# Feed-forward's first layer by seven products instead of eight, on pairs of chunks

## The chip, the cores and the metric

The kernel runs on one core of a Trainium2 chip. The metric is the device time in microseconds of one execution; before the change it is 3593.21 us (median of three runs, 3593.11 to 3593.33).

## The reference

Two gated layers on a batch of 16 sequences of 256 rows, width 512; the context has 256 rows of width 256. All is float32. The first layer is a cross-attention of 16 heads and a routed feed-forward of 8 experts; the second a normed cross-attention of 16 heads and a plain feed-forward with 2048 hidden columns. The last of the four lines is the one that the change is about:

```python
x = x + jnp.tanh(g_xattn[0]) * _L0_xattn_ref(_layernorm(x), ctx_1024, ...)
x = x + jnp.tanh(g_ffn[0]) * _L0_ffn_ref(_layernorm(x), ...)
x = x + jnp.tanh(g_xattn[1]) * _L1_xattn_ref(_layernorm(x), ctx_1024, ...)
x = x + jnp.tanh(g_ffn[1]) * _L1_ffn_ref(_layernorm(x), ...)

def _L1_ffn_ref(x, proj1, proj1_bias, proj2, proj2_bias, gate_w):
    h = jax.nn.gelu(jnp.einsum('lne,he->lnh', x, proj1) + proj1_bias, approximate=False)
    return jnp.einsum('lnh,eh->lne', h, proj2) + proj2_bias
```

## The kernel before

Four stages run one after another, each a function with its own prefix on tile names: `a_` (cross-attention and routing, 0 to about 1490 us), `e_` (experts, to about 2110 us), `d_` (normed attention, to about 2866 us) and `f_` (the last feed-forward, to the end). Every product is made of three matmuls in fp32r (`three`): each operand is split in a high part (a cast to fp32r on ACT) and a low part (value minus high part, a subtraction on DVE or POOL), and high times high, low times high and high times low are summed in PSUM.

**The feed-forward** (`feed_forward`, from L2462) walks over 8 chunks of 512 rows (`CH`). The hidden layer has 16 tiles of 128 columns (`HC`). For tile j of a chunk, `hidden` makes x times w1, transposed, in one bank `f_hb` (4 blocks of the width times 3 matmuls of 128x512, L2571 to L2573), ACT applies the gelu into `f_h_f` (L2635) and casts the high part (L2637), DVE subtracts for the low part (L2676), and `out` adds the tile's share of the second layer to four banks `f_ob` (4 blocks of rows times 3 matmuls). So a tile is 24 matmuls. PE's order is hidden(j+1), out(j); each engine's queue is in program order, and semaphores tie the engines. Rows of the next chunk are normed and turned (16 transposes through `f_tb`, L2579) while the chunk runs. All weights stay in SBUF, split at the stage's start.

**The first stage** (from L69) is a pipeline of 256 heads' steps; a step is one call of `step(f, u)` on each engine, some 4.4 to 6 us long, 8 to a batch and a half of the heads, 16 to one turn of the loop. In a step PE makes the queries (`a_pj`), the scores (`a_sc`), the values (`a_avb`), the projection (`a_ob`) and last turns the probabilities of two steps ago into the single bank `a_ptb` (L574), for which it waits until DVE has taken the low part of what the bank held (`a_pt_lo`, L851). ACT casts `a_pt_hi` (L734) first, then the query (L729), the exponentials (L740) and `a_ot_hi` (L749), and last what the batch shares: x, keys, values, and in every eighth step the context (`a_ctx`, L765). POOL scales the probabilities (L815) and in every eighth step takes a root (L820). SP loads and stores rows. ACT's queue also issues stores of blanks to `x_sorted` (L773).

Of the kernel before, what the change touches and what calls it, by code (L numbers as in the profile page):

```python
# [9 lines left out]
ALU = mybir.AluOpType  # L10
ACT = mybir.ActivationFunctionType
AX = mybir.AxisListType
P = 128
# [11 lines left out]
SLOTS = 42 * 7 * P  # L25
MADE = (2, 3, 4, 5)
# [43 lines left out]
def gated_cross_attention_and_route(nc, x_in, x_half, x_out, xt_rows, ctx_rows, x_sorted, y_sorted, tile_table, table, tab_loaded, weights, slots, listed, w_gate, wkv, kv_made, kv_kept, ident, in_hi, in_lo, ctx_t, mask, gate, wq, wk, wv, wo,  # L70
# [13 lines left out]
    with ExitStack() as ctx:  # L84
# [106 lines left out]
        kv_ctx, kv_zero, kv_ready, kv_taken = [sem(f"kv_ctx{j}") for j in range(len(MADE))], sem("kv_zero"), sem("kv_ready"), sem("kv_taken")  # L191
        o_ready, o_free, x_stored = sem("o_ready"), sem("o_free"), [sem("x_stored0"), sem("x_stored1")]
# [108 lines left out]
        def all_steps(eng, step):  # L301
# [3 lines left out]
            with eng.Fori(1, half - 1) as i:  # L305
                for u in range(AHEAD, AHEAD + PAIR):
                    step((i, 1, half - 2), u)
            for u in range(AHEAD, AHEAD + PAIR):
                step((half - 1, half - 1, half - 1), u)
# [21 lines left out]
        def kv_out(n):  # L331
            return prob[:, n % 4].rearrange("p t s -> p (t s)")

# [38 lines left out]
        def _(sp):  # L372
# [43 lines left out]
            def step(f, u):  # L416
# [45 lines left out]
                for n in splits(f, u):  # L462
                    if SET + 3 <= n + 3 < 2 * SET:
                        load(n + 3)
                at_step = last_steps(f, u)
# [19 lines left out]
            all_steps(sp, step)  # L485
            for n in (*KV_MORE, *KV_REST[:2]):
                keep_kv(n)
# [208 lines left out]
        def _(act):  # L696
# [34 lines left out]
            def step(f, u):  # L731
# [28 lines left out]
                for bb in context(f, u):  # L760
# [4 lines left out]
                    nc.scalar.copy(ctx_hi, ctx_raw[:]).then_inc(c_hid, 1)  # L765
                for n in splits(f, u):
                    split(n)
                for to, first, steps in ((x_sorted, 1, FILL), (y_sorted, B // 2 + 1, FILL_LATER)):
                    if f[1] == first and f[2] > first and u in steps:
# [34 lines left out]
        def _(pool):  # L804
# [5 lines left out]
            def step(f, u):  # L810
# [14 lines left out]

                if f[1] == f[2] and PAIR * f[1] + u == 117:
                    pool.wait_ge(pj_ready, number[B - 1, "x1"] + 1)
                    nc.gpsimd.memset(ones, 1.0).then_inc(ones_set, 1)
# [826 lines left out]

def gated_normed_attention(nc, x_in, y_sorted, weights, slots, x_out, ctx_rows, kv_made, kv_kept, dca_hi, dca_lo, kv_dca, gate, ln_cols, ident, raw_in, raw_out, in_hi, in_lo, after, ahead, tag):
# [11 lines left out]
    with ExitStack() as ctx:  # L1668
# [15 lines left out]
        y_sb = sb("y_sb", [P, 2, TOPK, D])  # L1684
# [42 lines left out]
        ff_loaded, ff_x_loaded = [sem("ff_loaded0"), sem("ff_loaded1")], sem("ff_x_loaded")  # L1727
# [103 lines left out]
        def _(sp):  # L1831
# [1015 lines left out]
```

## Time and profile before

| | us |
|---|---|
| median of three runs | 3593.21 |
| the profiled execution's own time | 3592.75 |
| its span | 3590.8 |
| PE busy (share of the span) | 3500.4 (97%) |
| DVE, ACT, POOL busy | 2166.8, 1824.2, 1461.9 |

The mean granted clock is 0.991 of full speed. A row of the timeline gives the start, the duration, the engine, the line, the operation, what it writes and reads, and in square brackets the idle time of the engine before it and who ended it. `<-` stands between output and input.

### The profile page before, as it was taken

Reading aid. Unit: us, or ns where it says so; the run is one execution under the profiler, and the core shown is the slowest. Engines: PE = TensorE matmul, PEld = TensorE weight load, DVE = VectorE, ACT = ScalarE, POOL = GpSimd, SP = SyncE. Lnnn points to the kernel's source line nnn. Section 1 sums busy time; section 2 is a strip of 40 time slices with the busy share of each in tenths; the row PEclk is TensorE's granted clock in tenths of the full one; section 3 lists DMA queues with packets and bytes.
Section 4 is the critical chain, followed back from the end, with each engine's and each line's share of the span. In section 5 each row is a group of like instructions: output and inputs, shape, how many; then the busy total and the mean of one; then the engine's idle time right before and its main releaser. Section 6 shows DMA issues by size and latency. Waiting matters only on the chain. (4 is left out here: it accounts for less than half of the span.)

```text
span 3590.8 us, 65577 instructions
## 1 busy us (share of the span) xinstructions
PE 3500.4 (97%) x22678; PEld 3030.6 (84%) x22678; DVE 2166.8 (60%) x5435; ACT 1824.2 (51%) x4724; POOL 1461.9 (41%) x1484
## 2 busy tenths in 40 slices
PE   9999999999999999899999997999999899999999
PEld 8999999999999998699999985667777588888887
DVE  6666666656666666577777777787777542222221
ACT  5444454554444444455555554787777732222222
POOL 4333333443444444354455545777777430000000
PEclk9999999999999999999999998999999999999999
DMA  4466666325666664577777662222221120000000
GB/s 166 171 226 226 225 219 219 137 95 190 219 219 222 220 220 142 201 257 256 264 261 255 248 236 94 83 81 66 63 66 64 43 84 24 24 24 24 24 24 24
DMA packets 232438, 530.18 MB, mean 148 GB/s; under 512 B 12929, under 2 KB 29442, under 8 KB 228098
## 3 DMA queue, kind: packets, MB, share of 16 engines
q1 hardware_dynamic: 131714, 314.14, 25.4%
q10 hardware_dynamic: 90208, 179.32, 13.5%
q0 software_dynamic: 10272, 33.63, 2.8%
q8 instruction: 134, 2.20, 0.3%
q14 instruction: 110, 0.90, 0.1%
HBM read 273.28 MB, written 253.76 MB: 147 GB/s over the span
## 5 line engine op out<-in xcount | busy, mean ns | idle before, releaser
L815 POOL TENSOR_SCALAR a_prob<-a_prob,a_rinv 128x256 f32<-128x256 f32 x512 | 472.4, 934 | 827.7 <-DVE a_rinv L1021 827.4
L740 ACT ACTIVATE a_prob<-a_prob,a_low_bias 128x256 f32<-128x256 f32 x512 | 256.4, 502 | 465.9 <-DVE a_low_bias L1012 465.9
L2635 ACT ACTIVATE f_h_f<-f_hb,ff_consts 128x512 f32<-128x512 f32 x128 | 88.3, 690 | 456.1 <-PE f_hb L2573 452.1
L500 PE MATMUL a_pj<-a_xt,in_hi 128*128 128x256 f32 x1024 | 309.9, 303 | 0.1
L1326 POOL TENSOR_TENSOR e_act_hi<-e_act_f,e_zeros 128x256 fp32r<-128x256 f32 x128 | 181.6, 1419 | 310.8 <-DVE e_act_f L1541 310.8
L1340 PE MATMUL e_gb<-e_xt_hi,in_hi 128*128 128x256 f32 x1024 | 291.6, 285 | 3.0 <-DVE e_xt_lo L1520 3.0
L1341 PE MATMUL e_gb<-e_xt_lo,in_hi 128*128 128x256 f32 x1024 | 290.7, 284 | 0.0
L1342 PE MATMUL e_gb<-e_xt_hi,in_lo 128*128 128x256 f32 x1024 | 290.7, 284 | 0.0
L502 PE MATMUL a_pj<-a_xt,in_lo 128*128 128x256 f32 x1024 | 289.1, 282 | 0.0
L501 PE MATMUL a_pj<-a_xt,in_hi 128*128 128x256 f32 x1024 | 288.9, 282 | 0.0
L851 DVE TENSOR_TENSOR a_ot_lo<-a_avb,a_ot_hi 128x256 fp32r<-128x256 f32 x256 | 108.3, 423 | 256.7 <-ACT a_ot_hi L749 256.7
L2184 POOL TENSOR_TENSOR raw_in<-raw_in,d_rinv 128x480 f32<-128x480 f32 x256 | 254.8, 1015 | 0.0
L1520 DVE TENSOR_TENSOR in_lo<-raw_in,in_hi 128x1024 fp32r<-128x1024 f32 (+1 forms) x160 | 205.4, 1288 | 60.9 <-ACT in_hi L1424 60.2
L2088 ACT ACTIVATE raw_in<-d_sc,d_nmax 128x240 f32<-128x240 f32 x512 | 232.9, 478 | 0.0
L2098 ACT COPY d_pt<-d_ptb 128x512 f32<-128x512 f32 x256 | 154.4, 603 | 118.4 <-PE d_ptb L1983 118.4
L851 DVE TENSOR_TENSOR a_pt_lo<-a_ptb,a_pt_hi 128x512 fp32r<-128x512 f32 x256 | 175.5, 686 | 51.6 <-ACT a_pt_hi L734 36.0
L2653 POOL TENSOR_TENSOR f_rstd<-f_var,f_power 128x4 f32<-128x4 f32 x7 | 7.0, 1006 | 486.7 <-DVE f_var L2700 486.7
L500 PE MATMUL a_ob<-in_hi,a_ot_hi 128*128 128x512 f32 x512 | 202.6, 396 | 2.6 <-POOL in_lo L824 1.9
L501 PE MATMUL a_ob<-in_lo,a_ot_hi 128*128 128x512 f32 x512 | 202.3, 395 | 0.0
L1340 PEld LDWEIGHTS e_gb<-e_xt_hi,in_hi 128*128 128x128 f32 x1024 | 197.5, 193 | 4.5 <-DVE e_xt_lo L1520 3.6
L502 PE MATMUL a_ob<-in_hi,a_ot_lo 128*128 128x512 f32 x512 | 199.7, 390 | 0.0
L1341 PEld LDWEIGHTS e_gb<-e_xt_lo,in_hi 128*128 128x128 f32 x1024 | 197.5, 193 | 0.9
(455 smaller groups left out, 11362.2 us busy)
## 6 DMA issues: line engine op xcount, KB each, us to landing
raw_in<-in_w_gate SPq DMA_DIRECT2D x39, 2048.0 KB, 8.6
x_sorted<-a_spare ACTq DMA_DIRECT2D x42, 1792.0 KB, 6.5
y_sorted<-a_spare ACTq DMA_DIRECT2D x42, 1792.0 KB, 8.8
raw_out<-in_w_out SPq DMA_DIRECT2D x40, 1024.0 KB, 5.4
xt_rows<-a_xt SPq DMA_DIRECT2D x16, 1024.0 KB, 5.4
a_xt<-xt_rows SPq DMA_DIRECT2D x16, 1024.0 KB, 5.2
e_xg<-x_sorted SPq DMA_DIRECT2D x32, 512.0 KB, 9.3
y_sorted<-e_y_sb SPq DMA_DIRECT2D x32, 512.0 KB, 2.9
```

The lines of the kernel that those rows point to most:

```text
L500: nc.tensor.matmul(out, a_hi, b_hi, start=start, stop=False)
L501: nc.tensor.matmul(out, a_hi, b_lo, start=False, stop=False)
L502: return nc.tensor.matmul(out, a_lo, b_hi, start=False, stop=stop)
L740: e = nc.scalar.activation(prob[:, u % 4, t], prob[:, u % 4, t], ACT.Exp, bias=low_bias[:, u % 2, t:t + 1], scale=-1.0, accum_out=rsum[:, ...
L815: p = nc.gpsimd.tensor_scalar(prob[:, u % 4, t], prob[:, u % 4, t], rinv[:, u % 2, t:t + 1], None, ALU.mult)
L851: return nc.vector.tensor_tensor(out, raw_in, hi.bitcast(F32), ALU.subtract)
L1340: nc.tensor.matmul(out, a_hi, b_hi, start=start, stop=False)
L1341: nc.tensor.matmul(out, a_hi, b_lo, start=False, stop=False)
L1342: return nc.tensor.matmul(out, a_lo, b_hi, start=False, stop=stop)
L1520: return nc.vector.tensor_tensor(out, raw, hi.bitcast(F32), ALU.subtract)
L2088: e = nc.scalar.activation(p[:, j, t, DCA:], s[:, j, t * S + DCA:(t + 1) * S], ACT.Exp, bias=nmax[:, n % 2, 1, 2 * j + t:2 * j + t + 1], a ...
L2184: T(p[:, j, :, DCA:], p[:, j, :, DCA:], r[:, 1, 2 * j:2 * j + 2].unsqueeze(2).to_broadcast([P, 2, S - DCA]), ALU.mult).then_inc(p_done, 1)
```

## The change

It splits both matrices of the first layer in halves of rows, width and hidden columns and makes the eight half products with seven (the scheme of Strassen in Winograd's form): 7 products of half the width for a tile of two hidden tiles and two chunks. The stage walks over 4 pairs of chunks (`PAIRS`) and 8 tiles j (`JC`) of a pair. For each (pair, j) PE makes seven `product`s of 2 x 3 matmuls into four banks of the tensor `turned`; ACT copies the first from PSUM (`snap`), DVE makes seven additions (`hidden`), ACT four gelus. The hidden tiles of the pair's first chunk go to `out` between the products; those of the second chunk are kept in SBUF and go to `out` when the first chunk is done. Four operands made of sums of x (T1 to T4) are made once a pair: `sums` on DVE, high parts on ACT, low parts on POOL and DVE.

The seven operands of w1 are made in the first stage, in 16 units of 64 columns (`prepared`): SP loads at step 4, 9 or 14 of a turn of the loop, POOL makes four sums one step later, ACT casts two steps later, POOL subtracts three steps later, SP stores four steps later to the DRAM tensor `w1_ops`. Three units fall into each of the five turns of the loop and one into the steps before it; the sixth turn, which was in the loop, is now written out. In the feed-forward SP loads each operand tile of each (pair, j, product) from `w1_ops` into a ring of 8 places, two transfers of 128 KB; the first eight places are filled in the attention. There the piece of w1 that was split ahead is gone, and the rows of the second chunk are loaded and normed ahead. All loops of the feed-forward are written out.

The diff, cut to its core; its pieces are, in order, `prepared`, then SP (two loops), ACT and POOL (two loops) of the first stage, then SP's `load_op` and PE's `hidden` (removed), `product` and main loops of the feed-forward:

```diff
+        def prepared(f, u, after):
+            if f[2] < B // 2 - 2 and f[1] >= 1:
+                return [at(f, lambda k: 3 * k - 2 + (u - after - AHEAD) // 5)] if u - after in (AHEAD, AHEAD + 5, AHEAD + 10) else []
+            return [0] if f[2] == 0 and u - after == 12 else []
...
+                for n in prepared(f, u, 0):
+                        sp.wait_ge(part_lod, n)
+                    for h in range(2):
+                        sp.dma_start(part_raw[:, h], w1[:, :, bass.ds(n * UNIT + h * H1 // 2, UNIT)]).then_inc(part_loaded, 16)
+                for n in prepared(f, u, 4):
+                    sp.wait_ge(part_lod, n + 1)
+                    for h, rows_of in enumerate((part_hi, part_lo)):
+                        sp.dma_start(w1_ops.rearrange("o c p h n -> p (o c) h n")[:, :, h, bass.ds(n * UNIT, UNIT)],
+                                     rows_of.rearrange("p (a n) -> p a n", a=14)).then_inc(part_kept, 16)
...
+                for n in prepared(f, u, 2):
+                    act.wait_ge(part_link, 3 * n + 3)
+                        act.wait_ge(part_kept, 32 * n)
+                    for of, to in part_of:
+                        h = nc.scalar.copy(part_hi[:, to].bitcast(F32R), w_raw[:].rearrange("p a b -> p (a b)")[:, of])
...
+                for n in prepared(f, u, 1):
+                    pool.wait_ge(part_loaded, 32 * n + 32)
+                    nc.gpsimd.tensor_tensor(part_sum[:, 0], a21, a22, ALU.add)
+                    nc.gpsimd.tensor_tensor(part_sum[:, 2], a11, a21, ALU.subtract).then_inc(part_link, 1)
+                    ...
+                for n in prepared(f, u, 3):
+                    pool.wait_ge(part_hid, n + 1)
+                    for of, to in part_of:
+                        l = nc.gpsimd.tensor_tensor(part_lo[:, to].bitcast(F32R), w_raw[:].rearrange("p a b -> p (a b)")[:, of], part_hi[:, to], ALU.subtract)
...
+            def load_op(n):
+                sp.wait_ge(p_ready, n - RING + 1)
+                for half, room in enumerate((ahead.ring_hi, ahead.ring_lo)):
+                    sp.dma_start(room(slot).bitcast(F32), w1_ops[op, :, :, half, j * P:(j + 1) * P].rearrange("c p n -> p c n")).then_inc(ring_loaded[slot], 16)
...
-            def hidden(n, b, j):
-                for c in range(FC):
-                    mm = three(hb[j % 2][:], w_hi[of][:, c, cols], w_lo[of][:, c, cols], xt_hi[b][:, c], xt_lo[b][:, c], c == 0, c == FC - 1)
+            def product(p, j, i):
+                if n >= RING:
+                    pe.wait_ge(ring_loaded[n % RING], 32 * (n // RING))
+                if j == 0:
+                    wait_op(p, i)
+                if i < 4 and g:
+                    pe.wait_ge(added, ADDS * (g - 1) + (3, 6, 7, 5)[i])
+                elif i == 4:
+                    pe.wait_ge(snapped, g + 1)
+                elif i > 4:
+                    pe.wait_ge(added, ADDS * g + i - 4)
+                for c in range(2):
+                    mm = three(out, hi[:, c], lo[:, c], x_hi[i][:, c], x_lo[i][:, c], c == 0, c == 1)
...
+            turn(rows_next, ob)
+            for i in range(N):
+                product(0, 0, i)
+            for p in range(PAIRS):
+                for j in range(1, JC):
+                    for i in range(5):
+                        product(p, j, i)
+                    out(p, 0, 2 * j - 2)
+                    product(p, j, 5)
+                    product(p, j, 6)
+                    out(p, 0, 2 * j - 1)
+                out(p, 0, HC - 2)
+                out(p, 0, HC - 1)
+                for k in range(HC):
+                    out(p, 1, k)
...
```

In the last loop PE also turns rows at k 1 and 7 and makes products of the next pair's first tile at k 13 and 14. `part_of` are two spans, of 256 and 640 columns: one unit of 64 columns is 14 such pieces for the seven operands.

What stands in ACT's row in the first stage around the step in which the context is cast (`a_ctx`), before:

```order
L749 CAST a_ot_hi<-a_avb 128x256 [waits a_av_ready]
L761 REGISTER_ALU
L764 ISA [waits a_pj_ready,a_c_loaded0]
L765 CAST a_ctx<-a_spare 128x512 [waits a_c_kept]
L734 CAST a_pt_hi<-a_ptb 128x512 [waits a_t_ready]
```

and now, in the loop's step 16:

```order
L780 CAST a_ot_hi<-a_avb 128x256 [waits a_av_ready]
L795 REGISTER_ALU [waits a_pj_ready,a_c_loaded1]
L796 CAST a_ctx<-a_spare 128x512 [waits a_c_kept]
L798 ISA
L801 REGISTER_ALU [waits a_part_link]
L804 CAST a_w_raw<-a_w_raw 128x256 [waits a_part_kept]
L804 CAST a_w_raw<-a_w_raw 128x640
L765 CAST a_pt_hi<-a_ptb 128x512 [waits a_t_ready]
```

Between the context's cast and the cast of the turned probabilities ACT now waits for POOL's sums (`a_part_link`) and for the stores of the unit before (`a_part_kept`), and makes two casts. POOL one step earlier, step 15, before:

```order
L815 TENSOR_SCALAR a_prob<-a_prob,a_rinv 128x256 [waits a_r_done]
L815 TENSOR_SCALAR a_prob<-a_prob,a_rinv 128x256
L818 ISA
L820 TENSOR_TENSOR a_columns<-a_columns,a_power 128x2 [waits a_stat_link]
L812 REGISTER_ALU
L815 TENSOR_SCALAR a_prob<-a_prob,a_rinv 128x256 [waits a_r_done]
```

and now:

```order
L855 TENSOR_SCALAR a_prob<-a_prob,a_rinv 128x256
L858 REGISTER_ALU
L860 TENSOR_TENSOR a_columns<-a_columns,a_power 128x2 [waits a_stat_link]
L867 ISA
L870 TENSOR_TENSOR a_w_raw<-a_w_raw 128x128 [waits a_part_loaded]
L871 TENSOR_TENSOR a_w_raw<-a_w_raw 128x128
L872 ISA
L873 TENSOR_TENSOR a_w_raw<-a_w_raw 128x128 [waits a_part_link]
L874 REGISTER_ALU
L875 TENSOR_TENSOR a_w_raw<-a_w_raw 128x128 [waits a_part_link]
```

The four sums stand behind the root and ahead of the next scaling. SP's row in steps 8 and 9 of the loop now reads:

```order
L490 REGISTER_ALU
L493 DMA w_ops<-a_w_raw 128x14x64 [waits a_part_lod]
L493 DMA w_ops<-a_w_raw 128x14x64
L412 REGISTER_ALU
L415 ISA [waits a_c_lod]
L415 DMA ctx_rows<-a_ctx 128x1024
L488 ISA [waits a_part_lod]
L488 DMA a_w_raw<-in_w 128x4x64
L488 ISA
L488 DMA a_w_raw<-in_w 128x4x64
```

Of these ten rows only the context's store (L415; L396 to L399 before) was there; the stores of one unit stand ahead of it and the loads of the next behind it.

## Rows read from the trace of the kernel before

**Rows 1.** Page, part 1: busy us, share, instructions of each engine

```profile
PE 3500.4 (97%) x22678; PEld 3030.6 (84%) x22678; DVE 2166.8 (60%) x5435; ACT 1824.2 (51%) x4724; POOL 1461.9 (41%) x1484
```

**Rows 2.** Windows: busy us (instructions) of each engine, then clock, DMA share, GB/s

```profile
300.00:600.00 300.00, 300.00 (x2152) 280.58 (x2151) 190.72 (x603) 149.25 (x430) 107.23 (x116) 1.00 0.63 226
3000.00:3200.00 200.00, 200.00 (x905) 165.55 (x904) 52.22 (x90) 53.03 (x82) 2.01 (x2) 1.00 0.06 22
```

**Rows 3.** Timeline, PE, steady feed-forward: start, duration, engine, line, operation

```profile
2887.71 0.39 PE L2571 MATMUL f_hb<-in_hi 128*128 128x512 f32 x1
...
2893.15 0.39 PE L2571 MATMUL f_hb<-in_hi 128*128 128x512 f32 x1
```

**Rows 4.** Waits, 2880 to 3591 us: total, times, longest

```profile
ACT f_h_f L2635 <- PE f_hb L2573: 447.9, 124, 4.8
```

**Rows 5.** Lines by form, 2890 to 3591 us: busy, mean ns | idle before

```profile
L2635 ACT ACTIVATE f_h_f<-f_hb,ff_consts 128x512 f32<-128x512 f32 x125 | 86.2, 690 | 450.0 <-PE f_hb L2573 446.0 <-DVE dca_lo L2676 4.0
```

**Rows 6.** Timeline, start of the feed-forward, 2871 to 2885 us

```profile
2871.47 0.63 PE L2572 MATMUL f_hb<-in_lo,in_hi 128*128 128x512 f32 x1
2871.90 0.63 PE L2573 MATMUL f_hb<-in_hi,in_lo 128*128 128x512 f32 x1
...
2879.64 4.62 POOL L2657 TENSOR_TENSOR in_lo<-raw_in,in_hi 128x2048 fp32r<-128x2048 f32 x1 [8.94 <-ACT in_hi L2624]
...
2880.76 4.05 DVE L2676 TENSOR_TENSOR f_h_lo<-f_h_f,f_h_hi 128x512 fp32r<-128x512 f32 x1 [2.36 <-ACT f_h_hi L2637]
...
2884.86 0.50 PE L2571 MATMUL f_ob<-in_hi,f_h_hi 128*128 128x512 f32 x1 [0.39 <-DVE f_h_lo L2676]
```

**Rows 7.** Timeline, first stage, 551 to 556 us, four engines

```profile
552.04 0.62 ACT L765 CAST a_ctx<-a_spare 128x512 fp32r<-128x512 f32 x1
552.56 0.58 ACT L734 CAST a_pt_hi<-a_ptb 128x512 fp32r<-128x512 f32 x1
...
551.20 1.82 POOL L815 TENSOR_SCALAR a_prob<-a_prob,a_rinv 128x256 f32<-128x256 f32 x2 [5.42 <-DVE a_rinv L1021]
552.99 0.97 POOL L820 TENSOR_TENSOR a_columns<-a_columns,a_power 128x2 f32<-128x2 f32 x1
...
553.30 0.68 DVE L851 TENSOR_TENSOR a_pt_lo<-a_ptb,a_pt_hi 128x512 fp32r<-128x512 f32 x1
...
555.28 0.60 PE L574 MATMUL a_ptb<-ident,a_prob 128*128 128x128 f32 x4
```

**Rows 8.** Timeline, POOL and PE, first stage, two other steps

```profile
537.89 1.82 POOL L815 TENSOR_SCALAR a_prob<-a_prob,a_rinv 128x256 f32<-128x256 f32 x2 [4.29 <-DVE a_rinv L1021]
...
545.89 0.60 PE L574 MATMUL a_ptb<-ident,a_prob 128*128 128x128 f32 x4
...
564.53 1.82 POOL L815 TENSOR_SCALAR a_prob<-a_prob,a_rinv 128x256 f32<-128x256 f32 x2 [2.82 <-DVE a_rinv L1021]
...
571.67 0.60 PE L574 MATMUL a_ptb<-ident,a_prob 128*128 128x128 f32 x4
```

**Rows 9.** Lines by form, POOL, whole span

```profile
L1328 POOL TENSOR_TENSOR e_act_lo<-e_act_f,e_act_hi 128x256 fp32r<-128x256 f32 x128 | 148.6, 1161 | 10.0
L2197 POOL TENSOR_TENSOR raw_in<-raw_in,d_hrstd 128x512 f32<-128x512 f32 x64 | 67.6, 1057 | 11.3 <-DVE d_hrstd L1825 11.3
...
L2182 POOL TENSOR_TENSOR raw_in<-raw_in,d_rinv 128x64 f32<-128x64 f32 x128 | 56.9, 445 | 158.8 <-DVE d_rinv L2408 157.7 <-POOL d_x_sb L2206 0.3
```

**Rows 10.** DMA: 682 to 683.5 us (1 KB packets), 3000 to 3088 us

```profile
DMA packets 480, 0.55 MB, mean 365 GB/s; under 512 B 9, under 2 KB 471, under 8 KB 471
...
q1 hardware_dynamic: 480, 0.55, 104.8%
...
q1 hardware_dynamic: 1056, 2.10, 6.7%
```

**Rows 11.** DMA issues, 590 to 614 us: KB each, us to landing

```profile
x_sorted<-a_spare ACTq DMA_DIRECT2D x3, 1792.0 KB, 6.5
```

More of the change, by code:

```diff
@@ L25 @@
 SLOTS = 42 * 7 * P
+NUNITS = 16
 MADE = (2, 3, 4, 5)
@@ L2525, in all_chunks @@
-        def all_chunks(eng, chunk):
-            for b in range(2):
-                chunk(0, b, False, b == 0)
-            with eng.Fori(1, CHUNKS // 2 - 1) as i:
-                for b in range(2):
-                    chunk(i, b, False)
-            for b in range(2):
-                chunk(CHUNKS // 2 - 1, b, b == 1)
+        credit = sb("credit", [P, 2])
+        b1_sb, gate_t = ahead.b1_sb, ahead.gate_t
+        rows = [ahead.x_first, ahead.xn, raw_in[:, 0, :, 0:D], raw_in[:, 0, :, D:2 * D]]
@@ L2568, in _ @@
+            store(2 * PAIRS - 1, other(PAIRS - 1))
+            sp.wait_ge(x_stored[0], 16 * PAIRS)
+            for n in (1, 2):
+                sp.wait_ge(x_stored[n], 16 * (PAIRS // 2))
         @block.tensor
@@ L2643, in _, with split, snap, gelu_of @@
-            all_chunks(act, chunk)
+            def split(m):
+                act.wait_ge(w_loaded, 32 * m)
+                nc.scalar.copy(w2_hi[:, m - 1], w2_raw).then_inc(w_hid, 1)
+            def snap(g):
+                act.wait_ge(p_ready, N * g + 1)
+                if g:
+                    act.wait_ge(gelu_done, 4 * g)
+                nc.scalar.copy(part[0], lw[:, BANK[0]]).then_inc(snapped, 1)
+            def gelu_of(g, n):
+                p, j = divmod(g, JC)
+                act.wait_ge(added, ADDS * g + (1, 4, 6, 7)[n])
+                if p == 0 and j == 4 and n == 1:
+                    act.wait_ge(w_lod, 3)
+                to, of = ((part[3], part[3]), (kept[JC + j], part[1]), (part[2], part[2]), (kept[j], part[0]))[n]
+                tile = j + JC * (n in (1, 2))
+                nc.scalar.activation(to, of, ACT.Gelu, bias=b1_sb[:, tile:tile + 1]).then_inc(gelu_done, 1)
@@ L2659, in chunk, with low_op @@
[L2659 to L2669 removed]
+            def low_op(p, i):
+                for c in range(2):
+                    pool.wait_ge(op_hid, 10 * p + {T1: 5, T3: 7, T4: 9}[i] + c)
+                    T(x_lo[i][:, c], raw_of[i][c], x_hi[i][:, c].bitcast(F32), ALU.subtract).then_inc(op_lod_pool, 1)
@@ new lines, in residual @@
+            def residual(n):
+                to, loads = (0, n // 2) if n % 2 == 0 else (other(n // 2), n // 2 + 1)
+                if n:
+                    pool.wait_ge(rows_loaded[to], 16 * loads)
+                for t in range(TC):
+                    r = T(rows[to][:, t], rows[to][:, t], b2_sb[:], ALU.add)
+                r.then_inc(res_done, 1)
+            def root(n):
+                pool.wait_ge(link_done, 3 * n + 3)
+                T(rstd[:], var[:], power[:], ALU.pow).then_inc(root_done, 1)
@@ new lines, in normalize @@
+            def normalize(n, x, tiles):
+                if tiles[0] == 0:
+                    dve.wait_ge(root_done, n + 1)
+                for t in tiles:
+                    l = V.tensor_scalar(rows[x][:, t], rows[x][:, t], mv[:, t, 0:1], rstd[:, t:t + 1], ALU.subtract, ALU.mult)
+                if tiles[-1] == TC - 1:
+                    l.then_inc(xn_done, 1)
+            sums(0, T1)
+            sums(0, T2)
+            low_op(0, T2)
+            sums(0, T4)
+            sums(0, T3)
```

710 lines of the change are left out of this document (461 added, 249 removed).

## The prediction

> **What bounds the kernel now.** I read the page's busy line first: PE is busy 97% of the span, 3500.4 of 3590.8 us, the next engine 60% [rows 1]. So time comes from fewer matmuls, and is lost by making PE wait. Then the windows, to see which stages have room. In 300 to 600 us, the first stage, PE is busy 300.00 of 300.00; DVE 191, ACT 149, POOL 107 [rows 2]. There a helper may grow in the mean, but every microsecond by which one comes late is a microsecond of the end, since PE has no idle time to give back. In 3000 to 3200 us, the feed-forward, PE is again busy for all of it and DVE, ACT and POOL 52, 53 and 2 us; the DMA share is 0.06 [rows 2]. The timeline gives the rate: one tile, 24 matmuls, starts at 2887.71 and the next at 2893.15, 5.44 us, 0.2267 us a matmul [rows 3]. The waits say who waits: ACT's gelu 447.9 us for PE's `f_hb` [rows 4], and no stop of PE in the windows. The feed-forward is the matmuls' time.
>
> **The products.** Before, 8 chunks x 16 tiles x 12 matmuls = 1536. Now 4 pairs x 8 tiles x 7 products x 6 = 1344. The second layer and the 16 transposes of each chunk stay. 192 fewer x 0.2267 [rows 3] = **-43.5 us**. Both forms are 128x512, and the clock is at full speed in the whole window [rows 2].
>
> What is added beside them: for each of 32 (pair, j) seven additions on DVE, one copy and four gelus and casts on ACT. An addition that reads PSUM is not there; the nearest row is the subtraction `a_pt_lo`, one input in PSUM, same size, 0.68 us [rows 7]. 224 x 0.69 = 155 us on DVE. A first-half group of PE is 42 + 24 = 66 matmuls, 15.0 us; DVE has 7 additions, 2 low parts of the tiles for the first chunk and 2 for the second: 11 x 0.69 = 7.6 us. ACT has 5 operations of 0.69 [rows 5] and four casts of 0.6, 5.9 us. Both fit twice over. By latency: a product of 6 matmuls is 1.36 us, an addition 0.68 us and some 0.1 of signal, and a bank is asked for again three or four products later. I take 0; if one addition a group is missed by 0.3 us it is 32 x 0.3 = 10 us, the upper end.
>
> **The ring.** 224 operand tiles, each 2 transfers of 256 packets of 512 B. No row shows 512 B. 480 packets of about 1 KB took 104.8% of 16 engines for 1.5 us, 52 ns each; 1056 of 2 KB took 6.7% of 88 us, 89 ns [rows 10]. By a straight line 512 B is about 34 ns, bounds 26 (half of 52) and 52. A tile needs 512/16 x 34 = 1.1 us (0.8 to 1.7) and PE gives it 15.0/7 = 2.1 us in a first half, and none are asked for in most of a second half (eight lie ready). I take 0, since even the upper end is below 2.1.
>
> **The start of the feed-forward.** Before: PE takes up the first tile at half pace (0.43 us from one matmul to the next [rows 6]) and stops 0.39 us for `f_h_lo`, which took DVE 4.05 us beside POOL's 4.62 us split of 128x2048 [rows 6], plus a few tenths at the turn. Now four operands are made one after another, DVE's sums, ACT's cast, the low part on POOL or DVE, some 1.2 us each in turn, while PE has a product of 1.36 us for each: I count stops of 0.8 + 1.3 + 1.3 + 0.8 = 4.2 us against about 1. **+3**, from -1 (the stop for `f_h_lo` goes too) to +8 (matmuls stay at half pace for another 40, 40 x 0.2). In the later pairs the operands are made behind 12 `out`s.
> The row shows 4.05 us for a 128x512 subtraction that takes 0.68 elsewhere, while POOL works: the Trainium skill says in the GPSIMD Engine Reference, section Specifications, that GPSIMD shares its SBUF interfaces with VectorE, with contention where DVE has two SBUF inputs. That speaks against the change, which adds POOL work in the first stage and keeps DVE's two-input subtractions; by it each POOL sum of a unit may hold a DVE operation up by its own 0.5 us. It is inside the lateness counted below: DVE's `a_pt_lo` reads one input from PSUM.
>
> **The first stage: the weights' units.** A unit has a part on POOL, ACT and POOL again, at three consecutive steps; three units to a turn of the loop, 5 turns, 15 units and one before. What decides is who stands behind. ACT's two casts stand ahead of `a_pt_hi`, behind that is DVE's `a_pt_lo`, and PE's `a_ptb` waits for it.
>
> Where the context is cast too (step 16 of the loop), before: POOL's scaling ends 551.20 + 1.82 = 553.02, the root at 553.96; ACT's context cast starts 552.04, `a_pt_hi` 552.56, DVE's `a_pt_lo` runs 553.30 to 553.98, and PE asks at 555.28 [rows 7]: a margin of 1.3 us. Now the four sums of 128x128 follow POOL's root. Nearest rows: 0.445 us for 128x64, 1.057 for 128x512 [rows 9]; by a straight line 128x128 is 0.53. Four, with waits between, 2.2 us (1.8 to 4.2): ready at 556.2. ACT casts 256 and 640 columns; 128x512 takes 0.62 [rows 7], so 1.1 us with the fixed part twice: 557.3. `a_pt_hi` 0.58: 557.9. `a_pt_lo` 0.68: 558.6, against 555.28: 3.3 us, and about 0.5 for what `a_ot_lo`, queued behind on DVE, holds up. 3.8 x 5 turns = **+19** (12 to 30).
>
> At the other two places there is no root. Step 6: scaling ends 537.89 + 1.82 = 539.71, sums 541.9, casts 543.0, `a_pt_lo` 544.3; PE asks at 545.89 [rows 8]: hidden by 1.6 us. Step 11: 564.53 + 1.82 + 2.2 + 1.1 + 1.3 = 570.9, PE at 571.67 [rows 8]: hidden by 0.8. With the sums at the upper end (the 128x512 row, 4.2 us) both are late, by 0.4 and 1.2, 5 x 1.6 = 8 us.
>
> **The loads behind stores.** SP stores a unit at the step before the next one is loaded: 2 transfers of 1792 packets of 256 B, then the context's store, then the loads, 1024 packets of 256 B. Meanwhile ACT's queue sends 1792 KB of blanks, which land after 6.5 us [rows 11]. With 24 ns for 256 B (half the step below 34; bounds 13 and 52): stores 3584/16 x 24 = 5.4 us, loads 1.5, context 512 KB about 1.5, blanks 5 at the full rate of the row: 13.4 us of queue, and the sums ask some 10 us after the issue. Late by 2 to 4.5 us less the margin of 0.8: I take 2 a turn, **+10** (0 if the queues are served by turns and the load is let through; 7 x 5 = 35 at 52 ns).
> The rows have no packet under 1 KB in numbers. The Trainium skill, DMA: Bandwidth & Descriptors, Specifications, gives 512 B as the least transfer for line rate, and below it a read-modify-write; the change's stores are below. Twice the price for the stores would be an estimated 5 us more a turn, +25.
>
> **The rest.** The attention (`d_`) loses its w1 splits and gets the second chunk's norm: DVE about +3, ACT -2, beside PE's products: 0 (-2 to +3). The loops written out: 0, since PE's instructions are issued from the same queue; no row shows a cost of a longer program.
>
> **Sum.** 3592.75 - 43.5 + 3 + 19 + 10 = 3581.2 in the profile's own time, which was 0.46 below the median of the runs: **3582**.
>
> **Rivals.**
> *H, the first stage hides it.* PE's queue runs ahead of `a_ptb` little, but the sums may be cheaper or POOL may be earlier than in the turn I read. Then 5 to 15 us are left of 29: 3592.75 - 43.5 + 3 + (0 to 15) + 0.5 = 3553 to 3568. For it: 107 of 300 us on POOL [rows 2]. Against it: PE has no slack, and `a_pt_lo` has 1.3.
> *S, slower.* The stores of 256 B and the loads behind them make every unit late. POOL's sums then stand ahead of the next scaling, and all of the chain is late by the DMA. It decides from a lateness of 8 us more than my 2, at the two places behind a store in a turn: 10 x 5 us + 19 = 69, time 3592.75 - 43.5 + 3 + 69 + 0.5 = 3622. Range 3601 to 3630. For it: the share of DMA is already 0.63 there [rows 2]. Against: 0.37 is free, and a unit has 5 steps.
> *D, the ring bounds PE.* If a tile's load takes more than 2.1 us (over 67 ns a packet of 512 B, or 1.07 us for the issue of each transfer on SP), the gain shrinks by 224 x the excess: at 2.4 us 224 x 0.3 = 67 us less in the first halves, 3600 to 3640. Against: both packet rows.
> *N, the products do not shorten the stage*, since a product of six matmuls waits each time for its bank: four stops of 0.3 us in each of 32 groups, 38 us; 3592.75 - 43.5 + 38 + 32 + 0.5 = 3620. The margins above speak against.
>
> **Chances.** Forecast 0.50 (its own range 3568 to 3592), H 0.27, S 0.14, D and N together 0.09. What a measurement of this kernel can tell from no change is 0.2%, 7.2 us: faster is below 3586.0, slower above 3600.4. The forecast's case is below 3586 seven times in ten, 0.35, the rest within 0.2%; with H faster is 0.62; S and D and N give slower 0.18 (part of their 0.23 stays within); same 0.20. Range: 0.1 to be left out at each side: 3556 to 3606.
>
> **What would show it.** The stage from the first `f_` matmul to the end shortens by some 40 us. PE's idle time ahead of the transposes to `a_ptb`, released by DVE's `a_pt_lo`, is 3 to 4 us at step 16 in each of five turns and under 0.5 at step 6. POOL's wait for `part_loaded` exists at one or both places behind a store. PE's waits for the ring are nought, and it has four stops at the start of the feed-forward. The forecast is wrong if PE waits for `added` or `snapped` in the groups, or if the idle time at `a_ptb` is not by these three steps.

## The result: 0.2% slower, and where the time went

The median of eight runs is 3603.95 us (3597.51 to 3608.60) against 3594.69 us (3593.11 to 3599.43) of the kernel before on the same chip; the ratio of the runs is 1.0022, with a 95% interval of 1.0013 to 1.0031. The forecast was 3582 and faster; the range 3556 to 3606 holds the time. The profiled execution took 3598.05 us (span 3596.2), 5.3 more than that of before.

| | before | after |
|---|---|---|
| first matmul of the experts | 1498.89 | 1548.38 |
| first matmul of the feed-forward | 2870.91 | 2917.60 |
| end | 3590.8 | 3596.2 |
| first stage | 1498.9 | 1548.4 (+49.5) |
| experts and second attention | 1372.0 | 1369.2 (-2.8) |
| feed-forward | 719.9 | 678.6 (-41.3) |

The stage borders are rows of the timeline, of before and of after (start, duration, engine, line, operation, in brackets the idle time of PE and who ended it):

```profile
1498.89 1.33 PE L1352 MATMUL e_tb<-ident,e_xg 128*128 128x128 f32 x5 [8.23 <-DMA e_xg<-x_sorted]
...
2870.91 0.77 PE L2571 MATMUL f_hb<-in_hi 128*128 128x512 f32 x1 [4.68 <-DVE f_credit L2680]
```

```profile
1548.38 1.97 PE L1408 MATMUL e_tb<-ident,e_xg 128*128 128x128 f32 x8 [6.18 <-DMA e_xg<-x_sorted]
...
2917.60 3.65 PE L2683 MATMUL f_ob<-ident,rows_next 128*128 128x128 f32 x16 [4.39 <-PEq L67]
...
2927.29 0.50 PE L2676 MATMUL turned<-in_hi 128*128 128x512 f32 x1 [1.18 <-POOL in_lo L2882]
...
2930.24 0.50 PE L2676 MATMUL turned<-f_op_hi,in_hi 128*128 128x512 f32 x1 [1.28 <-POOL f_op_lo L2882]
...
2932.90 0.50 PE L2676 MATMUL turned<-f_op_hi,in_hi 128*128 128x512 f32 x1 [1.03 <-POOL f_op_lo L2882]
```

The last three rows are the stops at the start of the feed-forward, 3.5 us for the sums of x. PE makes 22486 matmuls in place of 22678, the 192 fewer that were forecast, and is busy 97% of the span as before. The windows of after, which answer to [rows 2] (us busy of PE, of its weight loads, DVE, ACT and POOL, then granted clock, DMA share, GB/s):

```profile
3000.00:3200.00 200.00, 200.00 (x901) 166.06 (x900) 97.72 (x158) 65.81 (x106) 20.77 (x16) 1.00 0.43 127
405.03:411.30 6.27, 6.27 (x46) 5.76 (x47) 4.38 (x18) 3.04 (x11) 2.62 (x3) 1.00 0.00 0
565.57:572.63 7.06, 6.63 (x46) 5.99 (x47) 5.24 (x18) 2.77 (x9) 1.83 (x2) 1.00 0.87 335
178.21:185.90 7.69, 7.69 (x46) 7.43 (x47) 5.41 (x19) 3.39 (x11) 2.12 (x3) 0.78 0.78 299
500.30:508.04 7.74, 7.74 (x39) 7.43 (x40) 4.90 (x19) 3.56 (x12) 3.54 (x4) 0.63 0.00 0
600.00:604.00 4.00, 4.00 (x20) 4.00 (x19) 2.75 (x9) 2.21 (x7) 2.10 (x2) 0.50 0.00 0
```

In 3000 to 3200 us PE is as full as before; DVE went from 52 to 98 us and the DMA share from 0.06 to 0.43, and neither is felt. The other windows are the 6 to 8 us behind a stop in the first stage: the column ahead of the DMA share is the granted clock, and it is 1.00 in two of them, 0.78 and 0.63 in two, and 0.50, the lower of the two levels (1.2 and 2.4 GHz), in 600 to 604 us. A mean between 0.50 and 1.00 is a share of the window at each level. Who waits there, in the waits of PE from 150 to 640 us (total, times, longest):

```profile
PE a_ptb L605 <- DVE a_pt_lo L907: 29.4, 10, 5.0
PE a_ob L531 <- DVE a_xo_sb L1093: 0.4, 1, 0.4
```

The kernel before has no wait of PE in this stretch. There are ten stops at `a_ptb`, two to a turn. One kind is at step 16; here that of turn 2 on four engines:

```profile
303.17 0.97 POOL L860 TENSOR_TENSOR a_columns<-a_columns,a_power 128x2 f32<-128x2 f32 x1
304.11 0.46 POOL L870 TENSOR_TENSOR a_w_raw<-a_w_raw 128x128 f32<-128x128 f32 x1
...
305.61 0.45 POOL L875 TENSOR_TENSOR a_w_raw<-a_w_raw 128x128 f32<-128x128 f32 x1
...
306.28 1.03 ACT L804 CAST a_w_raw<-a_w_raw 128x256 fp32r<-128x256 f32 x2 [3.45 <-POOL a_w_raw L875]
307.22 0.58 ACT L765 CAST a_pt_hi<-a_ptb 128x512 fp32r<-128x512 f32 x1
...
307.83 0.69 DVE L907 TENSOR_TENSOR a_pt_lo<-a_ptb,a_pt_hi 128x512 fp32r<-128x512 f32 x1 [4.27 <-ACT a_pt_hi L765]
...
308.66 1.09 PE L605 MATMUL a_ptb<-ident,a_prob 128*128 128x128 f32 x4 [3.06 <-DVE a_pt_lo L907]
```

Root to 304.1, four sums to 306.1, two casts to 307.3, `a_pt_hi`, `a_pt_lo` to 308.5, and PE, which asked at 305.6, goes on at 308.66. This is the chain that was forecast from [rows 7]. The other kind is at step 11, where ACT's casts wait for the sums that POOL makes at its step 10 (POOL and SP, turn 2):

```profile
256.67 2.27 POOL L880 TENSOR_TENSOR a_w_raw<-a_w_raw 128x256 fp32r<-128x256 f32 x2
...
271.73 0.46 POOL L870 TENSOR_TENSOR a_w_raw<-a_w_raw 128x128 f32<-128x128 f32 x1 [2.96 <-DMA a_w_raw<-in_w]
...
259.08 4.24 SPq L493 DMA_DIRECT2D w_ops<-a_w_raw  x2
263.63 3.39 SPq L415 DMA_DIRECT2D ctx_rows<-a_ctx  x1
267.25 1.89 SPq L488 DMA_DIRECT2D a_w_raw<-in_w  x2
```

The low parts are done at 258.9. SP issues the stores for 4.24 us and the context's store for 3.39, and gets to the loads at 267.25; POOL has waited 2.96 us for them when the first sum begins at 271.73.

Set against the kernel before transpose by transpose (the start of each `a_ptb` group in both traces), the five turns lost 46.4 us, each time at these two places, and nothing at step 6:

| turn | step 11: stop, loss there, loss in the next step | step 16: the same |
|---|---|---|
| 1 | 2.44, 2.60, 1.55 | 4.56, 4.72, 1.53 |
| 2 | 2.04, 2.21, 1.52 | 3.06, 3.20, 1.34 |
| 3 | 2.06, 2.21, 1.54 | 3.05, 3.21, 0.28 |
| 4 | 2.07, 2.23, 1.48 | 3.05, 3.21, 2.61 |
| 5 | 2.07, 2.23, 0.93 | 5.01, 5.15, 2.61 |

The stops are 29.4 us. Another 17.0 us, over a third, were lost besides: 1.6 at the place itself and 15.4 in the step behind. The rows say how:

```profile
405.61 0.28 PE L532 MATMUL a_pj<-a_xt,in_hi 128*128 128x256 f32 x1
405.73 0.28 PE L533 MATMUL a_pj<-a_xt,in_lo 128*128 128x256 f32 x1
407.32 0.42 DVE L907 TENSOR_TENSOR a_ot_lo<-a_avb,a_ot_hi 128x256 fp32r<-128x256 f32 x1 [1.14 <-ACT a_ot_hi L780]
407.80 0.38 PE L531 MATMUL a_avb<-a_pt_hi,a_v_hi 128*128 128x256 f32 x1
...
600.40 0.41 PE L532 MATMUL a_pj<-a_xt,in_hi 128*128 128x256 f32 x1
600.61 0.41 PE L533 MATMUL a_pj<-a_xt,in_lo 128*128 128x256 f32 x1
```

- The 1.6 us, 0.16 a stop, come from how idle time is counted. A matmul row of 128x512 lasts 0.39 us while the next one starts 0.23 us behind it; the idle time counts from the row's end, 0.16 us later than PE could have gone on.
- Behind a stop at the lower level, two matmuls of 128x256 start 0.21 us apart (600.40 and 600.61) in place of 0.12 (405.61 and 405.73), so that 0.44 of each microsecond at that level is lost. The eight windows with a clock under 1.00 hold 31 us of it, which makes 14 us; these eight steps lost 14.2.
- Behind a stop at 1.00 a second, short wait follows. At 405.03 us PE goes on, and starts `a_avb` 2.77 us later, at 407.80, where it takes 2.58 us in the kernel before. DVE has just finished `a_ot_lo`, at 407.74: the late `a_pt_lo` made the scores' work on DVE late, this the exponentials on ACT, these `a_ot_hi`, and this `a_ot_lo`. The idle column does not show it, since it fits into the modelled length of the matmul before it. That is the 0.28; in the 0.93 of turn 5 there is also the wait of 0.4 us for `a_xo_sb`. At the lower level PE comes to `a_avb` 3.8 to 4.7 us behind the stop, when `a_ot_lo` is long done.

So the lower level took 14.2 of the 17.0 us. At full clock these steps would presumably have met the short waits instead; with 0.28 and 0.93 for them as in the two windows at 1.00, what the level added is some 9.3 us. Of the remaining 3.1 us of the first stage 2.9 are at its end, where PE stops 3.3 us for `a_xn`.

### The profile page after: what moved, and what is told of

The parts are those of the page before. It is cut to its first block and busy times, and to the rows that moved or that the text cites. A ratio compares the mean times of both kernels' runs of the same rounds, so it can differ in the third digit from the quotient of the medians.

```text
span 3596.2 us, 66239 instructions
## 1 busy us (share of the span) xinstructions
PE 3472.0 (97%) x22486; PEld 3009.8 (84%) x22486; DVE 2305.9 (64%) x5653; ACT 1867.4 (52%) x4821; POOL 1587.6 (44%) x1633
## 3 DMA queue, kind: packets, MB, share of 16 engines
q8 instruction: 135, 2.21, 0.2%
## 5 line engine op out<-in xcount | busy, mean ns | idle before, releaser
L531 PE MATMUL a_pj<-a_xt,in_hi 128*128 128x256 f32 x1024 | 313.6, 306 | 0.1
L532 PE MATMUL a_pj<-a_xt,in_hi 128*128 128x256 f32 x1024 | 292.4, 286 | 0.0
L2962 DVE TENSOR_TENSOR raw_in<-turned,raw_in 128x512 f32<-128x512 f32 x224 | 151.9, 690 | 212.7 <-PE turned L2678 209.8
L2158 ACT ACTIVATE raw_in<-turned,d_nmax 128x240 f32<-128x240 f32 x512 | 233.1, 478 | 0.0
L532 PEld LDWEIGHTS a_pj<-a_xt,in_hi 128*128 128x128 f32 x1024 | 199.1, 194 | 0.0
L531 PEld LDWEIGHTS a_pj<-a_xt,in_hi 128*128 128x128 f32 x1024 | 198.4, 194 | 0.5 <-DVE a_k_lo L907 0.5
```

Source lines behind the costliest of these rows:

```text
L531: nc.tensor.matmul(out, a_hi, b_hi, start=start, stop=False)
L532: nc.tensor.matmul(out, a_hi, b_lo, start=False, stop=False)
L2158: e = nc.scalar.activation(p[:, j, t, DCA:], s[:, j, t * S + DCA:(t + 1) * S], ACT.Exp, bias=nmax[:, n % 2, 1, 2 * j + t:2 * j + t + 1], a ...
```

## The experiments

**Without the units.** Theory A was that the units' lateness costs the first stage what the table shows; its rival was that the written-out program or the feed-forward's transfers cost something everywhere.

```diff
 def prepared(f, u, after):
-    if f[2] < B // 2 - 2 and f[1] >= 1:
-        return [...]
     return [0] if f[2] == 0 and u - after == 12 else []
```

> The changed kernel without the 15 units of w1 in the first stage's five turns: no loads, sums, casts, low parts or stores of them there. The one unit of the first turn stays and fills a small w1_ops of 128 columns, from which the feed-forward's ring loads every tile (same packets, other data). Theory A (the units' lateness costs the first stage its 46 us, by 29 us of stops of PE at a_ptb and 17 us of matmuls at the lower clock behind them): PE stops at a_ptb under 1 us in 150 to 640 us, clock 1.00 there, profiled time 3598 - 46 = 3549 to 3554, and the runs less scattered than the 3597 to 3609 of the changed kernel. Rival B (the written-out program, or the feed-forward's new transfers, slow everything a little): above 3575.

Measured: 3551.64 us, median of four runs (3549.62 to 3557.94), 0.9877 of before (0.9859 to 0.9894). PE has no wait in 150 to 640 us:

```profile
150.00:640.00 490.00, 490.00 (x3521) 458.54 (x3519) 313.95 (x993) 243.73 (x701) 174.95 (x188) 1.00 0.63 227
2872.80:3551.30 678.50, 668.80 (x2992) 554.40 (x2992) 330.09 (x523) 227.78 (x358) 95.72 (x66) 1.00 0.40 122
```

The 15 units cost 3598.05 - 3553.13 = 44.9 us between profiled executions. The medians of this section stand beside other runs of the kernel before, 3597.44 for this one and 3594.69 for the result above, so against these the units cost 52 to 55 us. The second row is the feed-forward, 678.5 us, for the next comparison. The four runs are less scattered than the eight of the changed kernel, by 8 us in place of 11, and not by much: the kernel before gave 3590.63 to 3600.43 here, the slower runs with a mean clock of 0.988, the fastest with 0.991.

**Without the ring's loads.** In `units_off`, `load_op` returns at once and PE waits only for the first eight tiles; all later products use these.

> units_off with the feed-forward's ring left as the first eight tiles filled it: no more loads of operand tiles in the feed-forward, PE waits for none. If the ring is hidden, as its waits of 0 on PE say, the time from the first f_ matmul to the end is that of units_off, 678.5 us, within 1 us. If the 56 MB that it moves slow the stage in a way that no wait shows, it is shorter by more.

```profile
2872.20:3550.80 678.60, 668.79 (x2992) 554.43 (x2992) 329.94 (x523) 227.69 (x358) 95.67 (x66) 1.00 0.11 38
```

678.6 us with a DMA share of 0.11, 678.5 with 0.40. The ring is free; the term of 0 for it was right.

**The casts a step later.**

```diff
-for n in prepared(f, u, 4):   # SP, stores
+for n in prepared(f, u, 5):
-for n in prepared(f, u, 2):   # ACT, casts
+for n in prepared(f, u, 3):
-for n in prepared(f, u, 3):   # POOL, low parts
+for n in prepared(f, u, 4):
```

> The changed kernel with each unit's casts on ACT, low parts on POOL and stores one step later; loads and sums stay. All the work and all the transfers are there, the output is the reference's. Theory A (the stop comes from what stands behind the wait for the sums): at the time of the cast the sums are a step old, so only the 1.05 us of casts stand ahead of a_pt_hi, the stops fall from 29 to under 3 us and the low clock goes with them: 3552 to 3560. Rival C (the added traffic and the ports hold the engines up, wherever the casts stand): 3585 or more, stops go on. Rival E (the low parts, now a step later on POOL, make the next unit's loads later still, and the sums hold the scalings up): 3565 to 3585.

Measured: 3555.31 us, median of four runs (3553.16 to 3557.51), 0.9882 of the kernel before (0.9866 to 0.9899). It is below the kernel before, 3597.44 beside it, by 42 us, and below the 3603.95 of the changed kernel by 49, with all transfers and all work of the units in it:

```profile
150.00:640.00 490.00, 490.00 (x3521) 458.55 (x3520) 320.99 (x993) 255.15 (x729) 232.40 (x274) 1.00 0.79 262
...
203.45 0.46 POOL L875 TENSOR_TENSOR a_w_raw<-a_w_raw 128x128 f32<-128x128 f32 x1
...
205.26 1.04 ACT L804 CAST a_w_raw<-a_w_raw 128x256 fp32r<-128x256 f32 x2 [0.87 <-DMA w_ops<-a_w_raw]
```

PE is busy 490.00 of 490 us at a clock of 1.00, with a DMA share of 0.79, where `units_off` has 0.63. So neither the added traffic nor POOL's added work beside DVE costs PE anything in this stretch. The last sum begins at 203.45 and the casts at 205.26; ACT waits 0.87 us for the stores of the unit before and for no sum, and the next `a_pt_hi` is still in time. What cost 46 us was where the waits stood. Two of them moved here: with the stores a step later, the loads of the next unit also stand ahead of them on SP. The next kernel has that alone; the casts moved alone were not run.

**The loads ahead of the stores.**

```diff
-for n in prepared(f, u, 4):   # SP, stores
+for n in prepared(f, u, 5):
```

> The changed kernel with the stores of a unit issued behind the loads of the next one instead of a step ahead of them; all else the same. The loads of the sums of step 10 are no longer behind 4.3 us of issuing of stores on SP. Theory A: POOL's 2.96 us of wait at step 10 is gone, with it the 2.1 us stop of PE and the 1.5 us behind it, five times 3.6 = 18; at step 15 the 1.5 and 1.95 us of load waits go, about 3 + 2: 3598 - 23 = 3575 (3570 to 3582), with five stops of 3.05 us left. Rival F (the loads are late by the share of the DMA engines, not by the queue's order): no change in the stops, 3595.

Measured: 3581.92 us (3578.70 to 3585.50), 0.9958 of before (0.9941 to 0.9975), at the upper end of what was expected; the profiled run 3582.56. SP and POOL at step 11 of turn 2, and PE's waits:

```profile
250.59 0.37 SPq L415 DMA_DIRECT2D ctx_rows<-a_ctx  x1
253.42 1.80 SPq L488 DMA_DIRECT2D a_w_raw<-in_w  x2
255.39 4.92 SPq L493 DMA_DIRECT2D w_ops<-a_w_raw  x2
...
262.99 0.46 POOL L870 TENSOR_TENSOR a_w_raw<-a_w_raw 128x128 f32<-128x128 f32 x1
```

```profile
PE a_ptb L605 <- DVE a_pt_lo L907: 15.2, 5, 3.0
```

The loads are issued at 253.4, ahead of 4.92 us of stores, and POOL no longer waits. All five stops at step 11 are gone, all five at step 16 are 3.05 us, and 9.7 us are lost behind them (2.57, 1.54, 1.46, 2.64, 1.53), more than I gave. Rival F is out. Of the 42 us that `cast_later` is below the kernel before, this order of loads and stores alone gives 15.5 and the later casts the other 27.

**Wider packets for the stores.**

```diff
-sp.dma_start(w1_ops.rearrange("o c p h n -> p (o c) h n")[:, :, h, bass.ds(n * UNIT, UNIT)],
-             rows_of.rearrange("p (a n) -> p a n", a=14))
+sp.dma_start(w1_ops...rearrange("(u p h a) -> u p h a", u=NUNITS, p=P, h=2)[bass.ds(n, 1), :, h]..., rows_of)
```

> The changed kernel, with each unit's parts stored as one row of 3584 B per partition in place of 14 pieces of 256 B (256 packets for 3584 a unit); the pieces then lie elsewhere in w1_ops, so the feed-forward's first layer multiplies with other numbers, in the same time. If the 256 B packets make the stores dear (the Trainium skill, DMA: Bandwidth & Descriptors, Specifications, puts the least size for line rate at 512 B), the issues of the stores on SP fall from 4.3 to under 1 us, the loads come early, the stops of 2.1 us at step 11 go, and 15 to 20 us with them: 3578 to 3583. If the order of the queue alone holds the loads up (the context's store and the blanks), the stops stay: 3595.

```profile
255.51 1.67 SPq L493 DMA_DIRECT2D w_ops<-a_w_raw  x2
257.50 0.97 SPq L415 DMA_DIRECT2D ctx_rows<-a_ctx  x1
258.70 2.45 SPq L488 DMA_DIRECT2D a_w_raw<-in_w  x2
...
266.24 0.45 POOL L870 TENSOR_TENSOR a_w_raw<-a_w_raw 128x128 f32<-128x128 f32 x1 [1.11 <-DMA a_w_raw<-in_w]
```

Measured: 3584.46 us in one run, the kernel before beside it 3593.41. The stores' issues take 1.67 us for 4.24 and the context's store behind them 0.97 for 3.39; POOL waits 1.11 us for 2.96, and PE's stop at step 11 is 0.18 us in turns 2 to 5 (1.09 in turn 1). The time is 1.5 us above what was expected, and the issues did not fall under 1 us. The same 896 KB in packets of 256 B hold SP's queue up by 5 us more than in packets of 3584 B, which is what the Trainium skill's page leads one to expect (DMA: Bandwidth & Descriptors, Specifications: line rate from 512 B on); the trace does not show its read-modify-write, only the time. The order of the queue and the size of the packets are two ways to the same 2 us.

**Stops without the units.** The kernel before was delayed on ACT alone. A first version (`late_three`) had a wrong bound on the loop, so that none of its copies were made; it is one more run of the kernel before, 3591.83 us. Its expectation was:

> The kernel before the change, with a_pt_hi copied 10, 12 and 13 times more at steps 7, 12 and 17 of each of the five turns, so that PE waits at a_ptb without any transfer, POOL or DVE work more. By the margins of 3.7, 3.9 and 1.3 us and 0.48 us a copy PE should stop 1.1, 1.9 and 4.9 us, 39.5 us in all. Theory A (a long stop itself lowers the clock behind it): behind the 1.9 us stop 1.5 us more are lost and behind the 4.9 us stop 1.5 to 2.6, behind the 1.1 us stop less or nothing; 3593 + 39.5 + 15 to 22 = 3648 to 3656. Rival C (what was lost behind the stops came from the units' traffic and engine work): only the stops, 3631 to 3636, and a clock of 1.00 behind them.

The mended one:

```diff
+for m in range(extra[u]):     # ahead of the copy of a_pt_hi, ACT
+    nc.scalar.copy(pt_hi[:, (u - 3) % 2], ptb[:]...).then_inc(again, 1)
+    act.wait_ge(again, ...)
```

> The kernel before the change, with a_pt_hi copied 7, 8 and 9 times more (each copy waiting for the one before by a semaphore, some 0.7 us each) at steps 7, 12 and 17 of the six turns of the loop, so that PE stops at a_ptb with no transfer and no POOL or DVE work more. By the margins of 3.7, 3.9 and 1.3 us the stops should be about 1.1, 1.8 and 5 us. Theory A (a stop of PE itself is followed by matmuls at the lower clock): behind the stops near 2 and near 5 us another 1.5 to 2.6 us are lost, with a granted clock under 0.8 in the next 6 us; behind the short one less or nothing. Rival C (what was lost behind the stops came from the units' traffic and engine work): the loss is the stops alone and the clock stays at 1.00 behind them.

```profile
179.50:186.60 7.10, 6.64 (x47) 6.03 (x48) 5.25 (x18) 2.72 (x9) 1.83 (x2) 1.00 0.80 210
212.90:219.60 6.70, 6.70 (x39) 6.40 (x40) 4.37 (x18) 3.55 (x12) 3.06 (x4) 0.75 0.00 1
...
PE a_ptb L575 <- DVE a_pt_lo L859: 49.4, 24, 4.6
```

Measured: 3674.19 us in one run, the kernel before beside it 3593.41. Behind each of the six stops of 4.63 us the next step lost 1.57 to 2.66 us; the window from 212.9 us has the clock at 0.75 with no transfer at all (DMA 0.00). A clock of 0.75 over 6.70 us is 3.4 us at the lower level, which at 0.44 is 1.5 of the 1.57 lost there. Behind the stops of 1.81 us it lost 0.92 to 0.95, the clock stays at 1.00 (window from 179.5), and 0.4 of it is a short wait for `a_xo_sb`. Behind those near 0.9 us 0.28. So the clock falls behind a stop without the traffic; rival C is out. The sizes match those of the changed kernel.

> The same kernel and the same kind of delay, but 3 to 7 copies more at eight steps of each of the six turns (5, 7, 9, 11, 13, 15, 17, 19), so that PE stops eight times for some 1 us instead of once for 5. If the clock falls only behind a long stop, the loss is the sum of the stops (about 45 us) and the clock stays at 1.00 in 100 to 650 us. If any idle share brings it down, it falls here as well and the loss is half as much again (65 us or more).

```profile
PE a_ptb L575 <- DVE a_pt_lo L859: 71.6, 60, 2.7
...
137.00:242.00 105.00, 92.60 (x632) 82.51 (x632) 55.23 (x179) 66.10 (x168) 31.69 (x34) 1.00 0.52 189
242.30:249.80 7.50, 7.50 (x41) 6.96 (x42) 4.55 (x18) 4.04 (x13) 3.66 (x4) 0.79 0.65 245
```

Measured: 3696.57 us in one run, stops of 0.72 to 1.70 us and, not meant so, one of 2.6 to 2.7 in turns 2 to 6. Neither expectation holds. In 137 to 242 us, with ten stops of 0.72 to 1.70 us, the clock stays at 1.00: idle share alone (PE is busy 93 of 105 us) does not bring it down. It falls behind the 2.60 us stop (0.79, and 1.47 us lost). Yet, set transpose by transpose as above, the six turns lost 103.9 us for 71.6 us of stops. The three terms found in the changed kernel account for it: 60 x 0.16 = 9.4 for the counting, 6.7 in the five steps at the lower level, and 0.28 in each of the other 55 steps (0.43 in five), 16.2. With the stops that is 103.9. In these steps PE starts `a_avb` 2.76 to 2.93 us behind the stop in place of 2.58, in most of them 0.05 us after DVE's `a_ot_lo` ends.

**The casts behind `a_pt_hi`.** ACT's block of `prepared(f, u, 2)` at the end of a step becomes `prepared(f, u, 3)` between the casts of `a_pt_hi` and `a_q_hi`.

> The changed kernel with one thing moved: on ACT a unit's casts, with their waits, stand behind the next a_pt_hi instead of ahead of it, and so ahead of the query's cast a_q_hi. Loads, sums, low parts and stores stay. Theory A (what stands behind the wait pays): the stops at a_ptb go (29 us, and 17 behind them), and a_q_hi and a_q_lo are late instead, which PE asks for at a_sc some 1.8 us after a_ptb. From the changed kernel's rows: casts end 597.9, a_q_hi and a_q_lo 0.8 later, PE would ask at 596.1, so 2.6 us where the loads are late (steps 15 of turns 1 and 5), 0.6 in the other three, and next to 0 at step 10: 7 us of stops, at most 5 behind them: 3598 - 46 + 7 to 12 = 3559 to 3564. Rival G (each place on ACT is as tight): the stops move to a_sc unshortened, 3590 or more.

```profile
PE a_pj L531 <- DVE a_q_lo L907: 20.7, 5, 5.6
PE a_avb L531 <- DVE a_ot_lo L907: 7.4, 5, 1.5
PE a_sc L531 <- DVE a_q_lo L907: 6.7, 5, 3.2
...
177.78 0.45 POOL L870 TENSOR_TENSOR a_w_raw<-a_w_raw 128x128 f32<-128x128 f32 x1 [7.56 <-DMA a_w_raw<-in_w]
```

Measured: 3616.17 us in one run, the kernel before beside it 3597.42. I was wrong by more than 50 us, and rival G's number holds. The stops at `a_ptb` are gone, but PE waits 34.8 us for the query and, which I had left out, for `a_ot_lo` behind it; and POOL waits 7.56 us for the loads of step 10. The later casts make the low parts later, and these the stores that stand ahead of the loads on SP. With the stores behind the loads:

> The same, and the stores of a unit behind the loads of the next one. The loads are then on time, and only the 0.6 us at step 15 are left, 3 us in all: 3552 to 3556, as cast_later. The output of both is the reference's.

```profile
PE a_avb L531 <- DVE a_ot_lo L907: 7.4, 5, 1.5
PE a_sc L531 <- DVE a_q_lo L907: 3.5, 5, 0.7
```

Measured: 3579.08 us (3575.29 to 3582.45), 0.9951 of before (0.9934 to 0.9967), 25 us above the forecast. The 0.70 us for the query are there, near the 0.6 expected, and 1.48 us more for `a_ot_lo` in each turn: the late query delays the exponentials, and `a_ot_hi` stands behind these on ACT. One step more of distance gives all of it back; a place a little further on in the same queue does not. Of the 4.25 us that a turn still loses, 2.18 are these two stops; the clock behind them is 0.76, about 1.5 us.

## Why the prediction was right and wrong

- **The products and the start of the feed-forward**, -43.5 + 3 = -40.5: measured -41.3, with three stops of 3.5 us in all where four of 4.2 were forecast. Right. The additions (0.69 us each, PE never waits for one) and the ring at 0: right, the ring by an experiment.
- **The units at step 16**, 3.8 a turn: the chain was right. It stops PE 3.06 us a turn, 15.3 in all, where 3.3 was worked out from [rows 7]; the sums took 0.46 us each for 0.53. That the stops add up to 18.7 us, against +19, is luck: 3.5 of them are late loads in turns 1 and 5, which I had not named, in the place of the 0.5 a turn that I gave for `a_ot_lo`. That wait exists, but behind the stop, 0.28 us and only at full clock.
- **Step 6 hidden**: right, no loss. **The loads at step 11**, +10: stops of 10.7 us. Right in size. The cause was right in part: the loads are late behind the stores, but what holds them up is SP's issuing, 4.24 and 3.39 us, and moving or widening the stores takes it away.
- **The step that failed** is "3.8 x 5 turns = **+19**" together with "I take 2 a turn, **+10**": both price a late helper at the length of PE's stop. A stop is followed by more: 17.0 us behind 29.4 us of stops, 14.2 of it in the eight steps in which the granted clock was at its lower level for a part, 1.2 in the two steps at full clock, by a second wait, and 1.6 that the idle time leaves out. With this term 3581.2 + 17.0 = 3598.2 in the profile's own time, where 3598.05 was measured; that the two agree to 0.2 us is luck, since the differences of the next item and the 0.8 us that the feed-forward gained beyond its term cancel. The text had the half pace at the start of the feed-forward before it, [rows 6], and used it there alone.
- **The other stages at 0**: -2.8 and, at the two ends of the first stage, +3.1.
- **The median** is 5.9 us above the profiled execution, and that of before 1.9: the eight runs have mean clocks of 0.983 to 0.987. In the twelve profiled executions 1369.2 (the changed kernel) to 1377.4 us (`behind_pt`) lie between the first matmul of the experts and that of the feed-forward, stages that the versions hardly differ in. The traces' clock records have 41.4 us of the lower level there in the first and 59.8 in the second, and 18.4 x 0.44 is the 8.1 us between them; so a part of the scatter comes from these stages, and the profiled execution of the changed kernel was the shortest there. Its eight runs go the same way, 3597.51 and 3598.05 us at a mean clock of 0.987, those above 3606 at 0.983 to 0.985. In which stages the median's extra 4 us lie no run here settles.
- **Rivals.** H (the stage hides it) is wrong. S has the sign right and its mechanism in part: the loads are late behind stores of 256 B, by 1.5 to 3.4 us and not by more than 8. The median, 3603.95, lies in its range of 3601 to 3630, but by what followed the stops and not by that lateness. D is wrong by the ring's experiment, and N by PE's waits. The sentence of the Trainium skill (GPSIMD Engine Reference, Specifications) on the interfaces that POOL shares with DVE was worth nothing in the sum. No effect shows in `cast_later`: its first stage is full, and `a_pt_lo` takes 0.684 us there for 0.683 before. But that subtraction has one input in PSUM, and the page speaks of two in SBUF; so no run here tests it for the units.

## What to carry to other kernels

Where an engine is busy all the time, price a stop of it at more than its length: in these traces a stop of 1 us cost 1.4, one of 3 us 3.5 to 5.8, one of 5 us 6.2 to 7.8, by the clock behind it and by the next helper that it makes late. When work is slipped in between the steps of a full pipeline, look less at its duration than at what stands behind its waits on each queue, the one that issues the transfers among them, and leave a whole step between the engine that makes and the one that takes. Moving one such block moves all that is chained to it: follow it to the stores and the next loads before giving a number.

## What was not expected of the hardware

- Behind a stop of PE in a stretch that was full before and after, the granted clock stayed at 1.00 for single stops up to 1.81 us, was 0.78 behind four of five stops of 2.04 to 2.44 us, and 0.62 to 0.81 behind those of 2.6 to 5 us at `a_ptb`, but for two of 3.05 us (one in the changed kernel, one in `wide_stores`) with 1.00. Stops of the same 3.05 us in the changed kernel were followed by 1.00, 0.78 and 0.63, and so by 0.28, 1.34 and 2.61 us of loss; what decides it no run here shows. Two stops of 0.70 and 1.48 us within 3 us were followed by 0.76 as well, in all five turns of `behind_pt_load_first` and in two of three such pairs in `behind_pt`; behind the third the clock stayed at 1.00. It needs no transfer beside it. Where the clock fell, PE ran about 3 to 6 us at the lower level (0.78 over 7.69 us, 0.63 over 7.74), and a microsecond of it cost 0.44 us.
- Each stop, short ones too, cost some 0.44 us besides itself at full clock. That is this pipeline and its records and not the chip: 0.16 us that the modelled end of the last matmul covers, and 0.28 of a second wait, for `a_ot_lo`, that the idle time does not show.
- Issuing a transfer on SP is not of one price: two stores of 1792 packets took 4.24 us at one step and 1.26 at another, and the 512 KB store behind them 3.39 us in place of 0.37.
